# Expert layers of an audio tower in 64x64 tiles, and an output turned by VectorE instead of TensorE

## The reference, cut to what matters

```python
feat = jnp.mean(x, axis=0)
w = jax.nn.softmax(feat @ Wr + br, axis=-1)
h = jnp.einsum('bfd,edh->bfeh', x, W1) + b1
h = jax.nn.relu(_bn(h, g1, be1, m1, v1))
h = jnp.einsum('bfeh,ehk->bfek', h, W2) + b2
h = jax.nn.relu(_bn(h, g2, be2, m2, v2))
y = jnp.einsum('bfeh,ehd->bfed', h, Wo) + bo
return jnp.einsum('bfed,fe->bfd', y, w)
```

## Time and profile before

| what | value |
|---|---|
| median of three runs | 845.72 us (844.11 to 847.37) |
| span of the profiled execution, first to last instruction | 844.2 us |
| TensorE busy | 714.3 us, 85% of the span |
| VectorE busy | 591.4 us, 70% |
| ScalarE busy | 557.8 us, 66% |
| GpSimd busy | 245.5 us, 29% |
| mean granted TensorE clock | 0.927 of full speed |

### The profile page before, as it was taken

One profiled execution on the slowest core, in us unless ns is written; L12 is line 12 of the kernel. 1 busy time (PEld: TensorE's weight loads), 2 busy tenths in 40 slices (PEclk: granted clock), 3 DMA queues, 4 the chain that ended last, 5 costly groups with the idle time before them and its releaser, 6 DMA issues.

```text
span 844.2 us, 8762 instructions
## 1 busy us (share of the span) xinstructions
PE 714.3 (85%) x2950; PEld 267.8 (32%) x2950; DVE 591.4 (70%) x1007; ACT 557.8 (66%) x877; POOL 245.5 (29%) x184
## 2 busy tenths in 40 slices
PE   9898879679879878968987987776657999999997
PEld 5332433333333233334333323323223222222222
DVE  5646967978986797797898679757627555555554
ACT  5858598689778868968977886795731434343432
POOL 8002500650460264065046016416512101011010
PEclk9959979999997999999999799997958999999999
DMA  2100000000000000000000000000000000000001
GB/s 69 30 2 0 1 2 1 1 0 3 0 1 2 1 0 1 3 0 1 2 1 0 1 0 1 2 0 0 1 4 0 26 26 13 26 22 16 25 14 37
DMA packets 12213, 7.06 MB, mean 8 GB/s; under 512 B 3005, under 2 KB 11493, under 8 KB 12165
## 3 DMA queue, kind: packets, MB, share of 16 engines
q1 hardware_dynamic: 11093, 5.71, 2.5%
q0 software_dynamic: 768, 0.69, 0.3%
q10 hardware_dynamic: 304, 0.07, 0.0%
HBM read 2.27 MB, written 4.19 MB: 8 GB/s over the span
## 4 chain that ended last, share of the span: by engine, by line
PE 40%; DVE 27%; ACT 26%; issue 4%; POOL 2%; DVEq 0%; POOLq 0%
PE TB L705 9%; PE TB L771 7%; PE QB L984 7%; DVE Z L1039 5%; DVE HH L1120 4%; PE QB L778 4%; PE TB L778 3%; ACT U L456 3%; DVE NN L1172 3%; PE TB L696 3%; DVE NC_ L1130 2%; ACT UF L464 2%; DVE M L1113 2%; DVE AT L1055 2%; ACT UF L466 2%
## 5 line engine op out<-in xcount | busy, mean ns | idle before, releaser
L705 PE MATMUL TB<-U,w2T 128*128 128x512 f32 x448 | 230.1, 660 | 49.6 <-ACT U L456 48.2
L456 ACT ACTIVATE U<-Z 128x512 f32<-128x512 f32 x192 | 114.4, 628 | 71.6 <-DVE Z L1039 71.3
L1039 DVE TENSOR_TENSOR Z<-TB,A 128x512 f32<-128x512 f32 x224 | 142.2, 681 | 23.3 <-PE TB L705 23.0
L677 ACT ACTIVATE A<-TB,bn_t 128x512 f32<-128x512 f32 x114 | 72.2, 684 | 124.1 <-PE TB L771 124.0
L705 PEld LDWEIGHTS TB<-U,w2T 128*128 128x128 f32 x448 | 89.0, 208 | 178.2 <-issue 88.0
L367 POOL TENSOR_TENSOR RSL<-HR,RSL 128x512 f32<-128x512 f32 x16 | 23.3, 1473 | 241.6 <-ACT RSL L555 241.6
L771 PE MATMUL TB<-XN,fw 64*128 64x512 f32 x256 | 73.6, 652 | 3.6 <-ACT A L474 2.7
L1327 DVE SCALAR_TENSOR_TENSOR Z<-TB,t_neg,AT 128x512 f32<-128x512 f32 x56 | 39.5, 746 | 47.0 <-PE TB L778 47.0
L428 POOL TENSOR_TENSOR SQ<-HH,LF_UT 128x512 f32<-128x512 f32 x16 | 21.6, 1352 | 171.4 <-DVE XC_IS L1336 155.4
L1327 DVE SCALAR_TENSOR_TENSOR Z<-QB,t_neg,AT 128x512 f32<-128x512 f32 x58 | 40.9, 746 | 34.1 <-PE QB L778 34.1
L984 PE MATMUL QB<-Z,fwo 128*64 128x512 f32 x118 | 63.2, 617 | 0.5 <-DVE Z L1327 0.5
(11 more groups left out here) (227 smaller groups left out, 1240.6 us busy)
## 6 DMA issues: line engine op xcount, KB each, us to landing
result<-V SPq DMA_DIRECT2D x32, 128.0 KB, 1.8
XN<-in_ffn_v SPq DMA_DIRECT2D x2, 256.0 KB, 4.9
XN<-in_ffn_g SPq DMA_DIRECT2D x2, 256.0 KB, 6.5
X<-in_x SPq DMA_DIRECT2D x8, 32.0 KB
fw<-in_ffn_W POOLq DMA_DIRECT2D x2, 128.0 KB, 2.9
fw<-in_ffn_W POOLq DMA_DIRECT2D x2, 64.0 KB, 2.6
fwo<-in_ffn_Wo POOLq DMA_DIRECT2D x2, 64.0 KB, 2.4
fwo_sw<-in_ffn_Wo POOLq DMA_DIRECT2D x2, 64.0 KB, 2.7
```

Of the source, the lines that this page charges most:

```text
L456: nc.scalar.activation(U3[:, 2 * j:2 * j + 2, 1:UW], Z3[:, 2 * j:2 * j + 2, :], ACT.Relu)\
L677: nc.scalar.activation(H1[t % 2][:, k, :], TB[k][:, :], ACT.Relu, bias=bn_t[:, 0, t % EP:t % EP + 1]).then_inc(b["h1"], 1)
L705: pe.matmul(TB[j][:, :], w2T[:, :], U3[:, 2 * j:2 * j + 2, 0:T], start=True, stop=True)\
L1039: nc.vector.tensor_tensor(Z[:, tc(j)], TB[j][:, :], A[:, tc(j)], ALU.add).then_inc(s["mix_add"], 1)
```

## The change

It has four parts. (1) `experts_in` is issued as four matmuls of 64 by 64. (2) `l3` is issued as four matmuls of 64 by 64, the products of half r of the rows into bank QB[r], so that the two experts' results lie in two banks. (3) `finish` adds both banks, in two dependent instructions. (4) `turn_out` is gone: VectorE transposes RES in blocks of 32x32 (one instruction, one step earlier in its queue than the copies were), and the output is stored by four DMAs for a block, each of 32 partitions in runs of 32 floats (128 bytes). The flags `last` and `last_late` are also formed otherwise; in the pass that runs here they have the same values.

```diff
-        OUTT = [V[:, 512 * f:512 * f + 512].rearrange("p (s n c) -> p s n c", s=2, n=2) for f in range(2)]
+        OUTT = [V[:, 512 * f:512 * f + 512] for f in range(2)]
...
-            ov = out.rearrange("(g s f n) (p r) d -> g s f p n (r d)", g=G, s=2, f=2, n=2, r=2)
+            ov = out.rearrange("(g s f n) (b i) (e j) -> g s e f i n b j", g=G, s=2, f=2, n=2, i=32, e=2)
             with sp.Fori(0, G) as g:
                 for f in range(2):
-                    for k in range(2):
-                        sp.wait_ge(b["tr_out"], 4 * g + 2 * f + k + 1)
-                        sp.dma_start(ov[bass.ds(g, 1), k, f].rearrange("a p n c -> (a p) n c"),
-                                     OUTT[f][:, k]).then_inc(stored[f], 16)
+                    sp.wait_ge(b["tr_out"], 2 * g + f + 1)
+                    for q in range(4):
+                        sp.dma_start(ov[bass.ds(g, 1), q // 2, q % 2, f].rearrange("a i n b j -> (a i) n b j"),
+                                     OUTT[f][32 * q:32 * q + 32, :].rearrange("i (n b j) -> i n b j", n=2, j=32))\
+                            .then_inc(stored[f], 16)
...
-                after(pool, b["res"], F - 1)
+                after(pool, b["res"], 2 * F - 3)
...
             def experts_in(t, banks, done):
-                for k in range(2):
-                    F, r = t // EP, k ^ (t // EP % 2)
-                    pe.matmul(banks[k][:, :], fw1[half[r], t % EP, :], XN2[half[r], HC * F:HC * F + HC],
-                              start=True, stop=True)\
-                        .then_inc(done, 1)
+                F = t // EP
+                for i in range(2):
+                    for k in range(2):
+                        r, e = k ^ (F % 2), k ^ i
+                        mm = pe.matmul(banks[k][half[e], :], fw1[half[r], t % EP, D * e:D * e + D],
+                                       XN2[half[r], HC * F:HC * F + HC], start=True, stop=True)
+                        if i == 1:
+                            mm.then_inc(done, 1)
...
                 if p == 0:
-                    after(pe, b["res"], F)
+                    after(pe, b["res"], 2 * F)
                 pe.wait_ge(b["hw"], 2 * t + 2)
                 src = H2_AHEAD[t] if t < N_AHEAD else H2[t % 2]
-                for k in range(2):
-                    mm = pe.matmul(QB[0][half[k], :], (fwo, fwo_sw)[k][:, p, :], src[:, k, :],
-                                   start=(p == 0), stop=(p == EP - 1))
+                for i in range(2):
+                    for r in range(2):
+                        k = r ^ i
+                        mm = pe.matmul(QB[r][half[k], :], (fwo, fwo_sw)[k][half[r], p, :], src[half[r], k, :],
+                                       start=(p == 0), stop=(p == EP - 1))
...
-            def turn_out(F):
-
-                pe.wait_ge(b["res"], F + 1)
-                after(pe, b["tr_out"], 2 * F)
-                for n in range(2):
-                    for r in range(2):
-                        mm = pe.transpose(QB[1][:, P * (2 * n + r):P * (2 * n + r) + P],
-                                          RES[F % 2][:, T * n + r:T * n + T:2], ident[:, :])
-                mm.then_inc(b["tr_mm"], 1)
...
             def finish(F):
                 dve.wait_ge(b["l3_mm"], F + 1)
                 dve.wait_ge(b["res_a"], F + 1)
-                after(dve, b["tr_mm"], F - 1)
                 nc.vector.tensor_tensor(RES[F % 2], QB[0][:, :], R1[F % 2], ALU.add).then_inc(b["res"], 1)
+                dve.wait_ge(b["res"], 2 * F + 1)
+                nc.vector.tensor_tensor(RES[F % 2], QB[1][:, :], RES[F % 2], ALU.add).then_inc(b["res"], 1)
 
             def token_major(F):
-                dve.wait_ge(b["tr_mm"], F + 1)
-                after(dve, stored[F % 2], 32 * (F // 2))
-                for k in range(2):
-                    nc.vector.tensor_copy(OUTT[F % 2][:, k].rearrange("p n (r d) -> p (n r) d", r=2),
-                                          QB[1][:, :].rearrange("p (m k d) -> p m k d", k=2, d=D)[:, :, k, :])\
-                        .then_inc(b["tr_out"], 1)
+                dve.wait_ge(b["res"], 2 * F + 2)
+                after(dve, stored[F % 2], 64 * (F // 2))
+                nc.vector.transpose(OUTT[F % 2], RES[F % 2]).then_inc(b["tr_out"], 1)
```

More of the change, by code:

```diff
@@ L217, in build @@
             "lg_mm", "mx", "nmx", "ex", "rc", "wn", "wb", "w_mm", "w_out", "wt_mm", "wt_out", "bo_mm", "bo_out",
-            "ws_out", "l1_mm", "h1", "l2_mm", "h2", "hw", "l3_mm", "res_a", "res", "tr_mm", "tr_out")}
+            "ws_out", "l1_mm", "h1", "l2_mm", "h2", "hw", "l3_mm", "res_a", "res", "tr_out")}
         stored = [sem("b_stored0"), sem("b_stored1")]
@@ L307, in _ @@
                     load_x(g).then_inc(x_in, 16)
-            ov = out.rearrange("(g s f n) (p r) d -> g s f p n (r d)", g=G, s=2, f=2, n=2, r=2)
+            ov = out.rearrange("(g s f n) (b i) (e j) -> g s e f i n b j", g=G, s=2, f=2, n=2, i=32, e=2)
             with sp.Fori(0, G) as g:
                 for f in range(2):
-                    for k in range(2):
-                        sp.wait_ge(b["tr_out"], 4 * g + 2 * f + k + 1)
-                        sp.dma_start(ov[bass.ds(g, 1), k, f].rearrange("a p n c -> (a p) n c"),
-                                     OUTT[f][:, k]).then_inc(stored[f], 16)
+                    sp.wait_ge(b["tr_out"], 2 * g + f + 1)
[3 more added lines that the diff above has]
+                            .then_inc(stored[f], 16)
             for f in range(2):
-                sp.wait_ge(stored[f], 16 * 2 * G)
+                sp.wait_ge(stored[f], 64 * G)
         @block.gpsimd
@@ L485, in turn @@
                 gm, ga, gl = (it - G, a - G, l - G) if plain else (it, a, l)
-                last = isinstance(it, int) and it == G
-                last_late = isinstance(it, int) and it == G + 1
+                last = it == G and not plain
+                last_late = it == G + 1 and not plain
                 if plain:
@@ L1003, in _ @@
                 l3(t)
-            turn_out(0)
             for t in range(N_AHEAD + 1, N_T + 2):
@@ L1010, in _ @@
                 l3(t - 2)
-                if t % EP == 3:
-                    turn_out((t - 2) // EP - 1)
-            turn_out(2 * G - 1)
         @block.vector
@@ L1352, in _ @@
                     finish(0)
-                if t == EP + 2:
+                if t == EP + 1:
                     token_major(0)
@@ L1358, in _ @@
                     finish(t // EP - 1)
-                if t % EP == 2:
+                if t % EP == 1:
                     token_major(t // EP - 1)
```

## The result

The changed kernel takes 818.16 us (median of four runs, 816.16 to 819.29), beside 845.62 us for the kernel before in the same session (844.11 to 847.37). The ratio is 0.9677, with a 95% interval of 0.9656 to 0.9699. The profiled execution took 817.78 us with a span of 816.0, so 28.2 us less than the span before. The forecast was 818 us.

A forecast was written before the change was run, and what follows sets the result against it. From 653 us to the end, TensorE's queue was taken as the bound. Start -0.7, 54 steps with 14 stops -28.1 and end +1.0 make -27.8 us: span 816.4, median 818 us, range 809 to 830.

The forecast's parts named there:

- A step of 2.60 us: Expert stage: three equal 64x64 stages take 2.60 us a step instead of 3.09, with ends 2.565 and 2.70.
- A stop of 0.5 us a block: TensorE ahead of layer 3 with p = 0: stands still about 0.5 us a block for the second add.
- turn_out gone, 0.66 a block: TensorE's queue: without turn_out each block is 0.66 us shorter, all of it on the path.
- The middle: From layer 1 at 656.21 to 831.73: 54 steps and 14 stops take 147.4 us instead of 175.5, 28.1 less.
- The start: Before the step at 656.21: second add costs 0.7, missing turn_out and shorter stages give back 1.1 and 0.3; 0.7 us less.
- The end: From the last step's layer 1 to the span's end: 12.5 to 14.5 us instead of 12.5; 1.0 us added.
- The transpose, 0.7 us: VectorE's transpose of a block: 0.7 us, bounds 0.34 and 2.4, covered inside the run, counted once at the end.
- The stores, 32.5 ns a packet: Output stores: 128 packets an engine and block at 32.5 ns, bounds 8 and 65, take 4.2 us; hidden except at the end.
- rival 2: Output stores set the pace from 102 ns a packet; at 110 ns blocks take 14.1 us, 873 us in all; chance 0.07.
- Rival 1: TensorE's issue of 48 loads and matmuls bounds a step, at 60 ns each 2.9 us; 822 to 836 us; chance 0.12.
- Rival 3: Expert stage: change of shape is not what costs; steps stay 3.09 us, only turn_out's time goes; 837 us; chance 0.04.
- Rival 4: Expert stage better than forecast: steps of 2.565 us, adds ending 0.3 earlier; 810 us or below; chance 0.05.

The follow-up runs named there:

- the version with ScalarE's copy: The changed kernel, but ScalarE copies bank QB[1] to SBUF and the second add reads that copy; 818.02 us, ratio 0.9645.
- the version without stops: The version with ScalarE's copy, with GpSimd's add for a later block released by the second add instead of the first; 808.75 us, ratio 0.9556.

## Why the prediction was right

Point by point, against the spans of the two profiled executions:

- **A step of 2.60 us** with ends 2.565 and 2.70. Measured 2.575. The relu is too late for the weights to be loaded ahead, as written, but the 0.035 us taken for it are not there: a step behind the stop, with half of its weights loaded ahead, takes 2.58 us as well (663.38 to 665.96). The half of the reason that carries the gain, that the price hangs on the change of shape, is shown by the runs that put one shape back: 2.93 and 2.89.
- **A stop of 0.5 us a block** for the second add, ends 0.3 and 0.7. Measured 0.48, released by L1329, in each of the 14 blocks. The second add ends 3.81 us after the start of layer 2 (658.61 to 662.42), forecast 3.9.
- **turn_out gone, 0.66 a block.** Measured on its own: 10.9 us at the median, of which 9.2 is this sum; the rest is within what these runs spread.
- **The middle**: forecast 147.4 us, measured 145.76. The sum there was 1.6 short of the gain: 54 x 0.025 = 1.35 for the step, the rest the stops.
- **The start**: forecast 0.7 less, measured 1.5 more. This is the term that failed, by 2.2 us. The sum took the clock of the profile before for granted, and TensorE's clock at 636 to 644 us may be 1.2 or 2.4 GHz; at 1.2 the stretch up to the copy on L1340 takes 3.2 us more (above). The mechanism that was forecast, adds later and stages shorter, agrees with the profile that has 2.4 GHz there: its step begins at 655.71, 0.5 less than before. In the profile of before it was 2.4 there:

```profile
636.00:640.00 4.00, 3.18 (x13) 1.93 (x14) 3.88 (x7) 2.32 (x3) 0.00 (x0) 0.96 0.00 0
640.00:644.00 4.00, 3.02 (x15) 0.78 (x13) 4.00 (x5) 0.00 (x0) 2.96 (x2) 1.00 0.00 0
```

- **The end**: forecast 1.0 more, measured none (803.51 to 816.0 is 12.5 us, as before). The adds and the transpose end within 0.1 of the forecast. What was mis-sized is the packet: 20 to 32 ns were taken for the end, and they take 12.9. They are done in the time that SP needs to issue the four DMAs.
- **The transpose, 0.7 us.** Measured 0.70, so the add was the right neighbour.
- **The stores, 32.5 ns a packet** with ends 8 and 65. Measured 12.9, near the lower end. The conclusion, hidden, held with much room: rival 2 began at 102 ns, eight times the measured price. The time to landing stayed at 1.8 us (median), as in the earlier trace rows.

```profile
L315 SPq DMA_DIRECT2D result<-V x64: 315/348/711, 654.2 to 813.8; - x64
...
DMA to landing us min/median/max: 1.7/1.8/3.4
```

In all: +1.5, -29.8 and 0.0 against the forecast's -0.7, -28.1 and +1.0. The total of -28.2 against -27.8 is that close because these errors, +2.2, -1.7 and -1.0, cancel; that is luck. The step, the stop, the transpose and the packet each lie inside their ends, and the end of the program lies on its lower one (12.5 us). The start had been given no bounds.

**Rival 1**, TensorE's issue, falls: 48 loads and matmuls go through in 2.575 us, 54 ns each, over 54 steps in a row, and the waits put to issue in the waits view are on the load side with no gap between matmuls. The Trainium skill's 62 ns for a matmul decoded in firmware (TensorE: Matmul & The Clock Gate, Back-to-back issue gap) cannot hold here for loads and matmuls alike: 48 of them would take 3.0 us, and a step takes 2.575. For the 24 matmuls alone it would be 1.5 us and no bound, and no run here tests that. **Rival 2** falls with 12.9 ns. The Trainium skill (DMA: Bandwidth & Descriptors, Specifications) has 512 B as the least for line rate and says that below it a transfer is done as read-modify-write. The first half agrees: by the byte an engine is busy 0.063 ns at 512 bytes, 0.10 at 128 and 0.14 at 64. A short packet that costs more than a long one, as the prediction's upper end had it, did not show, neither at 128 nor at 64 bytes. **Rival 3** falls with the two shape runs. **Rival 4**, steps of 2.565 and adds earlier, was half right on the step and wrong on the adds.

## What to carry to other kernels

When TensorE's queue is the bound, compare the pitch of a stage between neighbours of its own tile shape with its pitch between others: the difference is paid at every change of shape, and splitting a wide tile into equal narrow ones that run side by side is free if it makes the shapes the same. A layer split over two accumulation banks needs two reads, and the second becomes the wait ahead of the next accumulation; look for an engine with room to empty it. And when such work is moved, look at what the instruction now reads and who else works in that moment: two SBUF inputs beside GpSimd took back most of the gain in the steps (1.5 us were left of 6.7), and all of it in the median, until GpSimd's turn was moved as well.

## What the runs showed of the hardware

- **Two SBUF inputs beside GpSimd.** The same 128x512 add takes 0.69 us with one input in PSUM, GpSimd at work or not (661.73 above, with GpSimd from 661.77), 0.69 us with both inputs in SBUF and GpSimd idle, and 1.80 us with both in SBUF and GpSimd adding. In the source view of the version with ScalarE's copy most of its sixteen are slow (the median is 1,796 ns), and in the version without stops none, in this order:

```profile
L1340 DVE TENSOR_TENSOR XC_IS<-EO,XC_IS x16: 693/1796/1802, 650.2 to 809.6; 128x512 f32<-128x512 f32 x16
```

```profile
L1340 DVE TENSOR_TENSOR XC_IS<-EO,XC_IS x16: 692/693/693, 653.5 to 807.8; 128x512 f32<-128x512 f32 x16
```

  (min/median/max in ns.) The Trainium skill (SBUF — State Buffer, Who interferes with whom) says that a tensor_tensor with both inputs in SBUF comes into conflict with GpSimd's reads, over a shared read interface, and one with a single SBUF input does not. All three numbers agree. The weigh pair of the earlier trace rows is likely the same thing: in the first steps weigh reads SBUF only, and in the profile of before such a pair takes 2.42 us beside GpSimd's adds and 1.40 when GpSimd stands still (GpSimd works from 641.04 to 644.42 and from 647.64 to 649.35):

```profile
645.56 1.40 DVE L1327 SCALAR_TENSOR_TENSOR H<-H,t_neg,AT 128x512 f32<-128x512 f32 x2
...
647.49 2.42 DVE L1327 SCALAR_TENSOR_TENSOR RS_FS<-RS_FS,t_neg,AT 128x512 f32<-128x512 f32 x2
```

  No run moved GpSimd's adds there, so this rests on the timeline alone.
- **The change of shape.** Among its like a stage has a pitch of 0.86 us. Behind another shape it is 0.90 to 0.91, ahead of one 0.97, and between two it is 1.01 to 1.06, in both shape runs. The Trainium skill (TensorEngine Tiling (Array Packing), Key Properties) says that changing the tiling mode drains TensorE. The traces agree in that every change of shape lengthens the pitches around it; the drain itself is not seen in them. These are its prices with 512 columns of float32.
- **The clock at the stage's start** differs between executions of the same kernel: 1.2 GHz from 636 to 644 us in one profile, 2.4 in the other, ahead of it in both 627 to 636 us at 0.50 with TensorE busy 6.26 and 5.94 of 9 us. Up to the copy on L1340 it made 3.2 us, and 2.0 at the stage's first steps, behind another fall of the clock in both. What decides between the two is open.
- **The clock in the turns.** In the version with ScalarE's copy and the one without stops, the turns before the expert stage end some 3 us later than in the changed kernel, though no instruction of them was changed: the last matmuls that read UF start at 544.88 and 544.96 us, and at 541.16 and 542.01 in the two profiles of the changed kernel above. But the same differences stand between the two profiles of the changed kernel itself: the first matmuls that read UF start at 42.34 and 42.40, and at 41.78 (first profile) and 39.36 (second) in the changed kernel. The granted clock over the first 20 us is 0.83 in the two versions and in the first profile, and 0.91 in the second. From there on the turns take 502.5 us in both versions, 499.4 in the first profile of the changed kernel and 502.65 in the second. So the two versions have the longer time in both parts, and each profile of the changed kernel in one of them. Whether that is chance or has to do with the copy is open.
